# A fused attention and feed-forward kernel: the last stage's first loads, waits and batch order rearranged

## The reference

```python
x = x + cross_attention(ln(x), ctx, 16 heads, rms-normed q and k)
x = x + mixture_of_experts(ln(x), 64 experts, 8 per token, inner width 192)
s = where(mask, ln(x) @ ctx.T / sqrt(512), -1e30)     # per batch, 256 x 256
x = x + where(any(mask), softmax(s) @ ctx, 0)
n = ln(x)
x = x + (silu((n @ Wg.T) * gs) * ((n @ Wu.T) * us)) @ Wd.T * ds   # inner width 1408
```

## Time and profile before

| | us |
|---|---|
| median of the runs | 1503.74 |
| lowest and highest run | 1503.2, 1504.96 |
| profiled execution | 1498.16 |
| its span, first to last instruction | 1496.4 |
| last stage in it, from 1134.2 | 362.2 |
| PE busy, share of the span | 94% |
| mean granted PE clock | 0.966 of 2.4 GHz |

### The profile page before, as it was taken

One profiled execution on the slowest core, in us unless ns is written; L12 is line 12 of the kernel. 1 busy time (PEld: TensorE's weight loads), 2 busy tenths in 40 slices (PEclk: granted clock), 3 DMA queues, 4 the chain that ended last, 5 costly groups with the idle time before them and its releaser, 6 DMA issues.

```text
span 1496.4 us, 39189 instructions
## 1 busy us (share of the span) xinstructions
PE 1405.8 (94%) x8784; PEld 1194.8 (80%) x8785; DVE 1036.4 (69%) x2209; ACT 877.0 (59%) x2138; POOL 627.3 (42%) x727
## 2 busy tenths in 40 slices
PE   7999999999846999999999999999997899999998
PEld 5887766667625889888988998898885788888888
DVE  5555699976687777767777767667666666776732
ACT  5555699973356666666666766666652444344442
POOL 1222488861156222322333323222254766776322
PEclk9999999999955999999999999999998899999999
DMA  6221594001162788888778877778775745444100
GB/s 232 85 85 57 193 366 160 2 5 57 57 260 66 266 272 298 270 272 277 263 265 271 287 269 256 257 255 269 262 227 175 247 148 155 154 151 130 56 21 23
DMA packets 93134, 277.77 MB, mean 186 GB/s; under 512 B 12725, under 2 KB 12854, under 8 KB 92342
## 3 DMA queue, kind: packets, MB, share of 16 engines
q1 hardware_dynamic: 45910, 156.67, 30.5%
q0 software_dynamic: 23520, 77.09, 17.2%
q10 hardware_dynamic: 23616, 43.00, 7.7%
HBM read 208.55 MB, written 76.81 MB: 191 GB/s over the span
## 4 chain that ended last, share of the span: by engine, by line
PE 34%; issue 12%; DMA 5%; POOL 5%; ACTq 4%; ACT 4%; DVE 3%; DVEq 1%; SPq 0%; POOLq 0%
PE m_g L1400 14%; PE m_y L1420 8%; PE f_g L1894 5%; DMA y_rows<-y 4%; POOL G L1767 2%; POOL hT_low L1773 2%; PE f_y L1909 2%; PE m_x L1385 2%; ACT y L1601 1%; ACTq L1231 1%; ACTq L1605 1%; DMA raw_d<-in_exp_d 1%; PE f_sc L1848 1%; DVE X L1946 1%; ACT wgu_high L1121 1%
## 5 line engine op out<-in xcount | busy, mean ns | idle before, releaser
L1294 POOL DMA_INDIRECT xg<-h_rows,idx x160 | 163.2, 1020 | 431.6 <-PE m_x L1385 421.0
L1400 PE MATMUL m_g<-wgu_high,bxTh 128*128 x660 | 236.4, 358 | 6.8 <-DVE bxTl L1473 6.3
L1400 PE MATMUL m_g<-wgu_low,bxTh 128*128 x660 | 223.0, 338 | 0.0
L1400 PE MATMUL m_g<-wgu_high,bxTl 128*128 x660 | 222.9, 338 | 0.0
L1894 PE MATMUL f_g<-x4T_high,ffn_gu 128*128 128x256 f32 x704 | 176.9, 292 | 6.2 <-DVE x4T_low L2016 6.2
L1133 DVE TENSOR_TENSOR wgu_low<-raw_gu,wgu_high (+1 forms) x128 | 122.5, 959 | 86.8 <-ACT wgu_high L1121 66.7
L1894 PE MATMUL f_g<-x4T_low,ffn_gu 128*128 128x256 f32 x704 | 170.2, 283 | 0.0
L1121 ACT ACTIVATE wgu_high<-raw_gu (+1 forms) x128 | 108.0, 846 | 75.2 <-issue 73.8
L1420 PE MATMUL m_y<-wd_high,hidTm 128*128 x328 | 139.5, 425 | 5.7 <-issue 3.2
L1894 PEld LDWEIGHTS f_g<-x4T_high,ffn_gu 128*128 128x128 f32 x704 | 135.1, 192 | 11.8 <-issue 10.4
L657 POOL TENSOR_TENSOR prob<-prob,inv 128x512 f32<-128x512 f32 x128 | 130.6, 1042 | 24.8 <-DVE inv L603 23.0
(11 more groups left out here) (292 smaller groups left out, 3341.6 us busy)
## 6 DMA issues: line engine op xcount, KB each, us to landing
raw_gu<-in_exp_gu SPq DMA_DIRECT2D x64, 768.0 KB, 6.7
y_rows<-y ACTq DMA_DIRECT2D x164, 256.0 KB
raw_d<-in_exp_d SPq DMA_DIRECT2D x64, 512.0 KB, 7.5
y_rows<-zero SPq DMA_DIRECT2D x64, 256.0 KB, 3.4
ffn_gu<-ffn_gu_words SPq DMA_DIRECT2D x1, 5632.0 KB, 23.7
raw_c<-in_ctxT SPq DMA_DIRECT2D x16, 256.0 KB, 2.6
X<-in_x SPq DMA_DIRECT2D x4, 1024.0 KB, 5.5
h_rows<-h SPq DMA_DIRECT2D x16, 256.0 KB, 2.0
```

The lines of the kernel that those rows point to most:

```text
L1294: eng.indirect_dma_start(xg[:, u, :].bitcast(F32), None, h_dram, bass.IndirectOffsetOnAxis(ap=idx[half][:, u:u + 1], axis=0)).then_inc(s_g ...
L1400: m = eng.matmul(pg[u % 2][:, 0:2 * I], xT[l][:, u % 2, c, :], W.gu[r][:, buf * DC + c, :], start=c == 0 and n == 0, stop=c == DC - 1 and ...
```

## The change

- SyncE no longer issues the loads of memT, mask and mem for batch 0. ScalarE does, behind its last expert store and ahead of its first norm.
- GpSimd waits for `s_y` itself instead of for SyncE's `s_over`. It issues 12 of batch 1's gathers ahead of `deviations_4(0)`, not 14, then the other 4. Its gathers now run from one queue of places (`gather_next`): 1 for batch 2, then in batch 0 one behind each slice (two at f = 7), the other three behind the slices and 8 of batch 3; in batches 1 and 2 one behind each slice; from batch 3 on the old counts. `deviations_a(1)` stands before slice 3 of batch 0. At f = 7 (f = 10 in batch 0) the gather stands ahead of `deviations_4`, where it stood behind.
- VectorE: `read_in` and `moments_4` become `read_in_0` and `read_in_1`, one for each tile, each with its addition, statistics and aggregate. The last six additions of batch 1 and its moments stand beside slices 0 to 2 of batch 0. In batch 0 the additions for batch 2 stand at f = 4, 5, 7, 8, two each, two behind the last slice and six after `scales_4(1)`, and batch 1's `low` stands ahead of the store of tile 0.
- In batch 0 the steps of batch 1 stand before gate products 6, 7, 9 and 10 instead of 3, 4, 6 and 8, and `norm_3(1)` after silu 3 instead of silu 0.
- `keep_clock` does 12, 7, 13 and 5 matmuls instead of 8, 3, 8 and 2, and ScalarE does one silu of one column after `high_4(0)`.

```diff
@@ -1656,7 +1657,8 @@
-    GATHERS_2, GATHERS_3 = {0: 2, 1: 2, 2: 2, 3: 1}, {4: 1, 5: 1, 6: 1, 7: 1, 8: 1, 9: 1, 10: 2}
+    GATHERS_0, GATHERS_1 = {f: 1 + (f == 7) for f in fs}, {f: 1 for f in fs}
+    FIRST_ADDS, ADDS_0 = {0: (10, 12), 1: (12, 14), 2: (14, 16)}, {4: 2, 5: 2, 7: 2, 8: 2}
     with ExitStack() as held_here:
@@ -1672,6 +1674,7 @@
         ones, minus_half = sb("f_ones", [P, 1]), sb("minus_half", [P, TPB])
+        silu_first = sb("silu_first", [P, 1])
         Wdn = sb("ffn_d", [P, FC, D], F32R)
@@ -1691,7 +1694,7 @@
         dveA = Steps(nc, ctx, "f_dveA", [f"k{k}_{i}" for k in range(K) for i in TI] + each("st", "mv") + ["shift"])
-        dveC = Steps(nc, ctx, "f_dveC", ["neg"] + each("sc", "max", "nmax", "inv", "invv", "x", "st4", "mv4") + ["shift4"] + each("x4Tl"))
+        dveC = Steps(nc, ctx, "f_dveC", ["neg"] + each("sc", "max", "nmax", "inv", "invv") + [n + str(i) for i in TI for n in ("x", "st4", "mv4")] + ["shift4"] + each("x4Tl"))
         dveH = Steps(nc, ctx, "f_dveH", [f"h{f}" for f in fs])
@@ -1718,11 +1721,6 @@
             groups = used_groups(eng, endb)
-            added.wait(eng, 0, f"k{K - 1}_{TPB - 1}")
-            apart(eng, s_apart)
-            load_T(0)
-            eng.dma_start(open8[:, :, :], a["mask"].unsqueeze(0).to_broadcast([P, B, S])).then_inc(s_m, 16)
-            load(0)
             for u in range(2):
@@ -1786,36 +1784,41 @@
+            groups = used_groups(eng, endb)
             added.wait(eng, 0, f"k{K - 1}_{TPB - 1}")
...
             deviations_a(0)
-            eng.wait_ge(s_over, 1)
-            gather(1, places[:14])
+            for u in range(2):
+                eng.wait_ge(s_y[u], groups * 32 + 16)
+            apart(eng, s_apart)
+            gather(1, places[:12])
             deviations_4(0)
-            gather(1, places[14:])
-            gather(2, places[:4])
-            deviations_a(1)
-            gather(2, places[4:9])
+            gather(1, places[12:])
+            rows = deque((b, place) for b in range(2, B) for place in places)
+            def gather_next(last, n):
+                for _ in range(n):
+                    if rows and rows[0][0] <= last:
+                        b, place = rows.popleft()
+                        gather(b, [place])
+            gather_next(2, 1)
             for b in range(B):
-                n, of_2, beside = 0, 9, GATHERS if b > 0 else GATHERS_3
+                beside = GATHERS_0 if b == 0 else GATHERS_1 if b < 3 else GATHERS
                 for f in fs:
+                    if b == 0 and f == 3:
+                        deviations_a(1)
                     low(b, f)
-                    if b == 0:
-                        gather(2, places[of_2:of_2 + GATHERS_2.get(f, 0)])
-                        of_2 += GATHERS_2.get(f, 0)
-                    if b < B - 1 and f == 7 + 2 * (b == 0):
+                    gather_next(b + 3 if b > 0 else 2, beside.get(f, 0))
+                    if b < B - 1 and f == (10 if b == 0 else 7):
                         deviations_4(b + 1)
-                    if b < B - 3:
-                        gather(b + 3, places[n:n + beside.get(f, 0)])
-                        n += beside.get(f, 0)
-                if b < B - 3:
-                    gather(b + 3, places[n:n + 4])
+                gather_next(b + 2, 2 * K)
+                gather_next(b + 3, 4)
                 if b < B - 2:
                     deviations_a(b + 2)
-                if b < B - 3:
-                    gather(b + 3, places[n + 4:])
+                gather_next(b + 3, 4)
@@ -1864,26 +1867,27 @@
             added.wait(eng, 0, f"k{K - 1}_0")
-            keep_clock(8)
+            keep_clock(12)
             turn(0, "x3T", "n")
             scores(0)
-            keep_clock(3)
+            keep_clock(7)
             turn_probs(0)
...
             eng.matmul(py[0][0:1, 0:1], odd[:, :], ones[:, :], start=True, stop=True).then_inc(s_sum, 1)
-            keep_clock(8)
+            keep_clock(13)
             eng.wait_ge(s_exact, 1)
...
             turn(0, "x4T", "n4_")
-            keep_clock(2)
+            keep_clock(5)
             def gate_up(b, more, way, late):
-                beside = {1: lambda: turn(b + 1, "x3T", "n"), 2: lambda: scores(b + 1), 4: lambda: turn_probs(b + 1), 6: lambda: read(b + 1)}
+                steps = (lambda: turn(b + 1, "x3T", "n"), lambda: scores(b + 1), lambda: turn_probs(b + 1), lambda: read(b + 1))
+                beside = dict(zip((6, 7, 9, 10) if late else (1, 2, 4, 6), steps))
                 for f in fs:
-                    if more and f - late in beside:
-                        beside[f - late]()
+                    if more and f in beside:
+                        beside[f]()
                     if f < GUB:
@@ -1992,19 +1996,24 @@
-            def add_read(b):
-                for i in TI:
-                    dveC.wait(eng, b, f"invv{i}")
-                    peC.wait(eng, b, f"r{i}")
-                    t = b * TPB + i
-                    dveC.done(eng.scalar_tensor_tensor(X[:, t, :], px[i][:, :], inv[:, i:i + 1], X[:, t, :], ALU.mult, ALU.add), f"x{i}")
-            def read_in(b):
+            def read_in(b, i):
+                dveC.wait(eng, b, f"invv{i}")
+                peC.wait(eng, b, f"r{i}")
+                t = b * TPB + i
+                dveC.done(eng.scalar_tensor_tensor(X[:, t, :], px[i][:, :], inv[:, i:i + 1], X[:, t, :], ALU.mult, ALU.add), f"x{i}")
+                dveC.wait(eng, b, f"x{i}")
+                apart(eng, s_apart)
+                dveC.done(eng.bn_stats(stats4[:, i, :], X[:, t, :]), f"st4{i}")
+                dveC.wait(eng, b, f"st4{i}")
+                apart(eng, s_apart)
+                dveC.done(eng.bn_aggr(mv4[:, i, :], stats4[:, i, :]), f"mv4{i}")
+            def read_in_0(b):
                 inverses(b)
-                add_read(b)
-            def moments_4(b):
-                moments(b, dveC, "4", "x{}", dveC, stats4, mv4)
+                read_in(b, 0)
+            def read_in_1(b):
+                read_in(b, 1)
@@ -2048,26 +2057,25 @@
             eng.wait_ge(s_m, 16)
+            negatives(0)
             link(eng.tensor_reduce(valid[:, :], open8[:, :, :], axis=AX.X, op=ALU.max))
-            negatives(0)
             maxima(0)
...
             find_odd()
-            add(1, adds[:4])
-            read_in(0)
-            moments_4(0)
+            add(1, adds[:3])
+            read_in_0(0)
+            read_in_1(0)
             find_exact()
+            add(1, adds[3:4])
             scales_4(0)
-            add(1, adds[4:10])
+            add(1, adds[4:6])
             low(0)
-            add(1, adds[10:])
-            moments_a(1)
-            scales_a(1)
+            add(1, adds[6:10])
             eng.wait_ge(s_s, 48)
             def one(b, more, more2, late=0):
-                beside = {0: negatives, 1: maxima, 5: read_in, 6: moments_4, 8: scales_4}
+                beside = {5: negatives, 6: maxima, 9: read_in_0, 10: read_in_1} if late else {0: negatives, 1: maxima, 5: read_in_0, 6: read_in_1, 8: scales_4}
                 n = 0
@@ -2077,16 +2085,30 @@
                                                        ALU.mult, ALU.mult), f"h{f}")
-                    if more and f - late in beside:
-                        beside[f - late](b + 1)
+                    if more and f in beside:
+                        beside[f](b + 1)
+                    if late:
+                        if f in FIRST_ADDS:
+                            add(1, adds[slice(*FIRST_ADDS[f])])
+                        if f == 2:
+                            moments_a(1)
+                        if f == 3:
+                            scales_a(1)
                     if more2:
-                        add(b + 2, adds[n:n + ADDS.get(f, 0)])
-                        n += ADDS.get(f, 0)
+                        here = (ADDS_0 if late else ADDS).get(f, 0)
+                        add(b + 2, adds[n:n + here])
+                        n += here
+                if late:
+                    add(b + 2, adds[n:n + 2])
+                    n += 2
+                    scales_4(b + 1)
                 if more2:
...
                     moments_a(b + 2)
+                if late:
+                    low(b + 1)
                 store(b, 0)
-                if more:
+                if more and not late:
                     low(b + 1)
@@ -2144,12 +2166,18 @@
+            added.wait(eng, 0, f"k{K - 1}_{TPB - 1}")
+            apart(eng, s_apart)
+            eng.dma_start(memT[:, :, :], a["memT"][:, 0, :, :]).then_inc(s_memT, 16)
+            eng.dma_start(open8[:, :, :], a["mask"].unsqueeze(0).to_broadcast([P, B, S])).then_inc(s_m, 16)
+            eng.dma_start(mem[:, :, :], a["mem"][:, 0:TPB, :]).then_inc(s_mem, 16)
             for stage in (norm_3, turned_3, exps, turned_probs, norm_4, high_4):
                 stage(0)
+            eng.activation(silu_first[:, :], lnp4[:, 0, 0:1], ACT.Silu)
             eng.wait_ge(s_s, 48)
```

(8 more changed lines are left out.)

1 line of the change is left out of this document (added).

## The result

| | before | after |
|---|---|---|
| median of ten runs beside each other, us | 1505.14 | 1520.57 |
| profiled execution | 1498.16 | 1520.87 |
| its span | 1496.4 | 1519.1 |
| mean granted PE clock | 0.966 | 0.963 |

The changed kernel is slower: ratio 1.0085, 95% interval 1.0068 to 1.0102 (one disturbed execution of 3373 us is not in the ratio). The forecast was 1502.7, its range ended at 1508.8. It was wrong, and outside its range.

The account below looks back on a forecast made before the run. It took TensorE's own work, 39.4 us a batch, plus waits on the prologue's loads, GpSimd and VectorE as the bound. Terms -4.2, -1.9, +1.9 and +3.2 gave -1.0: 1503.74 to 1502.7 us, range 1495.5 to 1508.8.

Parts of the forecast that it names:

- Prologue, -4.2: Before batch 0's first gate product: earlier loads, full clock and changed fillers start batch 0 at 1162.3, 4.2 us sooner.
- a cost where they outlast the wait they fill: Prologue's longer keep_clock: 0.9 us lost between scores and turned probabilities, 1.7 before the later turn.
- silu_first: Prologue, ScalarE's early silu: takes one 1.28 us table load out of product 0's path, worth nothing.
- Loads: Prologue: ScalarE issues memT sooner, landing near 1139.5; scores start at 1141.25 instead of 1143.06, 1.8 us.
- Batch 0, -1.9: Batch 0, with the second batch's steps before later gate products: 47.6 us instead of 49.5.
- Batch 1, +1.9: Batch 1: low clock after TensorE's 5 us idle costs 2.8, less 0.9 of vanished stall; 44.4 us from 42.5.
- Batches 2 to 4, +3.2: Batches 2 to 4: GpSimd's changed order delays TensorE by 3.2 us in sum, bounds 0 and 8.3.
- The deviations behind the gather: GpSimd at product 7: scale 1.25 us later, 0.55 of it reaching x4T_low in each of batches 3 and 4.
- the new gathers: GpSimd, batches 1 and 2: next deviations 2.9 us later, 1.05 of it reaching TensorE in each of batches 2 and 3.
- By tile: Statistics made tile by tile on VectorE: 0 to +0.3 us a batch, hidden by GpSimd's lows.
- Rival 2: GpSimd's lag reaches TensorE whole at the x3T turns, 8.3 instead of 3.2: 1507.8; chance 0.24 with low-clock mixtures.
- The median: Whole kernel: the median of the runs lies 5.6 us above the profiled execution, forecast at 1497.2.

Follow-up runs that it names:

- after_3: The changed kernel unaltered, profiled a third time, on a chip where the kernel before had a median of 1506.7 us; ratio 1.0095 to the kernel before.
- before_3: The kernel before unaltered, a third profile, on a chip where the kernel before had a median of 1507.8 us; ratio 0.9990.
- after_again: The changed kernel unaltered, profiled once more, on a chip where the kernel before had a median of 1493.9 us; ratio 1.0051 to the kernel before.
- before_again: The kernel before unaltered, profiled once more, on a chip where the kernel before had a median of 1493.9 us; ratio 1.0002.

## Why the prediction was wrong, step by step

The forecast added -4.2, -1.9, +1.9 and +3.2 to -1.0. On a late chip (after_3 against before_3) the same terms are +1.2, +1.1, +4.0 and +5.3, together +11.6; on an early one (after_again against before_again) -4.0, +3.2, +4.4 and +4.6, together +8.2.

- **Prologue, -4.2.** Right on an early chip, 31.0 to 27.0, with the scores at the full clock and the first filler to the scores in 7.1 us, as the 7.06 of the forecast. On a late chip it is +1.2 (34.5 to 35.7). The step that failed there is "a cost where they outlast the wait they fill": it took the price of a filler row from a stretch at the full clock, 0.23 us, and saw no cost in them but their length. On late chips the first 24 rows took 5.8 to 8.5 us, where the forecast has 6.0, and the read, for which it had counted 0.9, came 5 to 7 later behind the scores than with the short fillers, behind late signals of TensorE. silu_first: worth nothing in every sum. The Trainium skill (ScalarE: Activation LUTs, What ACT_TABLE_LOAD costs) would add some 1.38 us to each switch; in after_again the load takes 1.28 us at 1156.86 and the silu starts at 1158.15, right behind. The trace disagrees, and the time hung on neither.
- **Loads.** Issue (0.7 us behind the last store) and landing (3.6 us later) right. That an earlier issue is the gain was wrong on a late chip, where beside the long fillers it is worth nothing; alone it shortened the prologue by 1.3 on an early one.
- **Batch 0, -1.9.** Measured +3.2 on the early chip (47.3 to 50.5), +1.1 on a late one. The x3T stall (1.90), its time (T+13.5 for T+14.3), and the idle of 5 us (5.06) were right (the forecast says some 2 us of stall, though its T+14.3 and T+11.7 make 2.6). What failed is an addition: between the turn and the scores stands product 6, 2.1 us at least, left out. Scores end at T+21.5, not T+19.6, gate products at T+33.1, not T+31, and batch 1 starts at T+49.4 to T+50.5, not T+47.6. And the 49.5 of before was itself a long one: four profiles of that order have 47.3 to 48.4.
- **Batch 1, +1.9.** Its start at 0.50 was right and smaller: 3.78 us for 16 rows against 2.14, so 1.6, less 0.8 of stall saved. Missed was down: 1.9 us of idle on hT_low and some 1.6 of low clock behind it, in all +4.3, not +1.9. The window behind that idle:

```profile
1268.50:1276.40 7.90, 7.90 (x33) 6.41 (x34) 6.09 (x12) 1.10 (x3) 6.31 (x8) 0.78 0.66 185
```

- **Batches 2 to 4, +3.2.** Measured +4.6 to +5.3. The deviations behind the gather were put at 1.1 and cost 2.9, batch 1 with them; the new gathers at 2.1, as waits for xn ahead of the x3T turns of batches 2 and 3, and cost 4.1, 2.8 of it in batch 1. x3T waited 0.3; down waited 1.4, 1.0 and 1.0 in batches 2 to 4. The failed step: it followed the new gathers beside products 8, 9 and 10 only to the next norm's deviations and from there to the turn of x3T, and put their cost on down at nothing, without a reason. GpSimd's last lows stand behind those gathers, and down needs them first. By tile: hidden, said the step; 0.25 a batch, say the runs.
- **Rival 2**, GpSimd's lag reaching TensorE whole, was nearer in size (8.3 and the 1.9 of batch 1's clock in its bounds, 9.0 measured for batches 1 to 4, clock in it) and had the wrong place: its sign, idle above 2.4 us ahead of x3T, never came, because the lag reached TensorE earlier, through h.
- **The median.** The profile of before (1498.16) lay 5.6 below its median, and the forecast carried that over as a constant. That profile has no stall in the experts' stage, and all twelve on late chips have; that the other runs of before had it is likely and not shown, as only profiled runs show stages. The difference of the two first profiles, 22.7, holds 10 us that the change did not make. What it did make is 7.6 us on an early chip (0.51%) and 13 to 14 on a late one (0.85%, 0.95%).
